# Residual adds shared out, Newton normalizers, a new meeting of two counting passes, and a causal mask added by VectorE behind the passes

## What is computed

```
h = relu(layernorm(x)); x = x + L0(h)   # two graph convolutions, then LSTMs over windows of 1, 2, 3, 4 nodes
h = relu(layernorm(x)); x = x + L1(h)   # graph attention: leaky scores, masked where adj == 0, softmax
h = relu(layernorm(x)); x = x + L2(h)   # attention: scores = q k^T * scale + adj, causal mask -1e30, softmax
h = relu(layernorm(x)); x = x + L3(h)   # U = eigenvectors of the normalized Laplacian of adj
                                        # out = U (relu(U^T h W1 + b1) W2 + b2)
```

## Time and profile before

| | us |
|---|---|
| median of 3 runs (879.49 to 884.33) | 883.62 |
| the profiled execution | 882.39 |
| its span, first to last instruction | 880.4 |
| TensorE busy / VectorE busy | 772.6 (88%) / 709.2 (81%) |
| ScalarE busy / GpSimd busy | 503.6 (57%) / 173.2 (20%) |
| granted TensorE clock, mean | 0.963 of full |

### The profile page before, as it was taken

One profiled execution on the slowest core, in us unless ns is written; L12 is line 12 of the kernel. 1 busy time (PEld: TensorE's weight loads), 2 busy tenths in 40 slices (PEclk: granted clock), 3 DMA queues, 4 the chain that ended last, 5 costly groups with the idle time before them and its releaser, 6 DMA issues. The chain is left out here.

```text
span 880.4 us, 13711 instructions
## 1 busy us (share of the span) xinstructions
PE 772.6 (88%) x3730; PEld 512.6 (58%) x3738; DVE 709.2 (81%) x3425; ACT 503.6 (57%) x1115; POOL 173.2 (20%) x398
## 2 busy tenths in 40 slices
PE   4699989999999999999999996688866887788998
PEld 3578854445445666665545545466645565566665
DVE  6888779999877889888888879778879899869433
ACT  0288956654443444444334331388755786698775
POOL 3111112222121221122122100012122322270000
PEclk9999999999999999999999999699997999899999
DMA  9100000000000000000000000000000000000122
GB/s 272 51 3 1 1 1 2 0 1 1 1 1 1 1 1 1 0 1 1 1 0 1 0 1 1 0 1 1 1 1 1 1 1 1 0 1 1 48 73 72
DMA packets 13970, 12.16 MB, mean 14 GB/s; under 512 B 1091, under 2 KB 10822, under 8 KB 13894
## 3 DMA queue, kind: packets, MB, share of 16 engines
q1 hardware_dynamic: 10992, 8.47, 3.3%
q10 hardware_dynamic: 2902, 2.82, 1.1%
HBM read 7.10 MB, written 4.19 MB: 13 GB/s over the span
## 5 line engine op out<-in xcount | busy, mean ns | idle before, releaser
L592 ACT ACTIVATE G<-bank,bias 128x512 f32<-128x512 f32 (+1 forms) x252 | 158.5, 633 | 181.5 <-PE bank L689 161.9
L689 PE MATMUL bank<-HT,wih 128*128 128x512 f32 (+1 forms) x504 | 246.0, 575 | 0.4 <-ACT HT L578 0.4
L441 POOL TENSOR_TENSOR col_root<-sa,neg_half 128x1 f32<-128x1 f32 x126 | 69.0, 548 | 409.6 <-DVE sa L936 409.6
L689 PE MATMUL bank<-H,whh 128*128 128x512 f32 (+1 forms) x288 | 137.6, 560 | 1.3 <-DVE H L934 0.8
L532 ACT COPY T<-bank 128x512 f32<-128x512 f32 x128 | 75.0, 586 | 55.2 <-PE bank L689 38.6
L528 ACT ACTIVATE T<-X,nbias,rstd 128x128 f32<-128x128 f32 x256 | 104.5, 484 | 3.0 <-DVE nbias L935 3.0
L689 PEld LDWEIGHTS bank<-HT,wih 128*128 128x128 f32 x504 | 81.0, 193 | 16.8 <-issue 10.2
L689 PEld LDWEIGHTS bank<-VI 128*128 128x128 f32 x254 | 45.0, 196 | 76.6 <-DVE VI L934 57.0
L689 PEld LDWEIGHTS bank<-XI,A 128*128 128x128 f32 x252 | 44.6, 197 | 57.4 <-DVE A L935 48.7
L699 PE MATMUL bank<-ident,T 128*128 128x128 f32 x256 | 40.9, 291 | 38.8 <-ACT T L635 32.6
L935 DVE SCALAR_TENSOR_TENSOR XI<-xy,bank 128x2 f32<-128x2 f32 x125 | 28.2, 225 | 43.3 <-PE bank L689 35.2
(11 more groups left out here) (350 smaller groups left out, 1664.9 us busy)
## 6 DMA issues: line engine op xcount, KB each, us to landing
out_x<-T SPq DMA_DIRECT2D x16, 256.0 KB, 2.3
wih<-in_WihT ACTq DMA_DIRECT2D x1, 1024.0 KB, 12.6
whh<-in_WhhT ACTq DMA_DIRECT2D x1, 1024.0 KB, 18.3
qkvT<-in_WqkvT ACTq DMA_DIRECT2D x1, 192.0 KB
wg<-in_Wg ACTq DMA_DIRECT2D x2, 64.0 KB
l3w<-in_L3W ACTq DMA_DIRECT2D x2, 64.0 KB
adj<-in_adj SPq DMA_DIRECT2D x1, 64.0 KB, 1.9
adjT<-in_adjT ACTq DMA_DIRECT2D x1, 64.0 KB
```

Source lines behind the costliest of these rows:

```text
L441: e.tensor_tensor(out=col["root"][:, :], in0=sa[:, 0:1], in1=neg_half[:, :], op=ALU.pow).then_inc(root_ready, 1)
L592: e.activation(G[x.h][:, gate, 0:n], gate_bank(k)[:, 0:n], ACT.Tanh if gate == 2 else ACT.Sigmoid, bias=bias[:, 4 * (x.p - 1) + gate:4 * ( ...
L689: mm = lambda out, l, r, start=True, stop=True: e.matmul(out, l, r, start=start, stop=stop)
```

## The change

- `half_list` has seven empty halves ahead in place of three, and no statistics in it. 45 attention halves are done by the end of the second pass, before and after.
- The residual adds: VectorE keeps groups 0, 3, 6, 9, 12 and 15. For the ten others ScalarE copies the bank to a tile of `T` and GpSimd adds that to `X`. VectorE takes `bn_stats` of all 16, in the order `RESIDUALS`. TensorE may turn the first groups before the last LSTM result stands. GpSimd's first tables now stand behind its ten adds.
- `normalizers` makes `rstd` on VectorE: an integer seed from the bits of the variance and three Newton steps. Statistics 3 to 7 use it; their square roots on ScalarE are gone. An exponential of one column in the residual stage (`warm`) loads ScalarE's table early.
- At the meeting of the passes one half is done ahead of the counts, one while TensorE forms the histogram, then statistics 4 and two halves ahead of step 0 of the second pass; the second pass has no place at step 2. The signs and sums of the first three blocks of each pass are put one slot later than `slot_of_block` gives, and within the slot ahead of the norm of a later group.
- For the nine groups whose scores come behind the passes (23 to 31) TensorE leaves out the mask product. VectorE makes, graph by graph, the negated sum of scores and `cmask` into `T`, with its minimum over the row as the bias; ScalarE's exponential reads `T` with scale -1.
- The parts of `tridiagonal` stand at other places among the last LSTM pieces.

The diff, cut to its core; its pieces are, in order, the lists, GpSimd's adds, ScalarE's copies and dropped roots, TensorE's mask product, and VectorE's functions.

```diff
-    halves = [("none", 0)] * 3
+    halves = [("none", 0)] * 7
...
+STATISTICS = {HALF.index(("scores", NG // 2 * m + 1)): m + 3 for m in range(1, 4)}
...
-    return 2 if step % n in places else 0
+    return 2 if step % n in places and (ps == 0 or step > n) else 0
...
+def on_vector(g):
+    return g % 3 == 0
+RESIDUALS = (0, 3, 1, 6, 2, 4, 9, 5, 7, 12, 8, 10, 15, 11, 13, 14)
+MASKED_BY_VECTOR = min(k for k in range(NG, GROUPS) if HALF.index(("scores", k)) >= block_ends()[-1] + 2)
-    BLOCKS_AFTER.setdefault(slot_of_block(_n), []).append(_n)
+    BLOCKS_AFTER.setdefault(slot_of_block(_n) + (_n % NB < NB - 1), []).append(_n)
...
+            for g in range(NG):
+                if not on_vector(g):
+                    xg = X[:, ds(g * GB, GB), :]
+                    e.wait_ge(st_c, copied_on_scalar(g))
+                    e.tensor_tensor(out=xg, in0=half4(turned_residual(g)), in1=xg, op=ALU.add).then_inc(st_g, 1)
...
+            def residual_copies(groups):
+                for g in groups:
+                    if not on_vector(g):
+                        e.wait_ge(st_T, g + 1)
+                        copy(turned_residual(g), bank[4 + g % 4], st_c)
+                if k == 1:
+                    e.activation(warm[:, :], half[:, :], ACT.Exp)
-            root(3)
-                if S in ROOTS_AFTER:
-                    root(ROOTS_AFTER[S])
-                if not it:
-                    root(7)
...
-                if nx:
+                if nx and nx.k < MASKED_BY_VECTOR:
                     mask = gmask if nx.gat else cmask
                     mm(half4(bk[2]), ident[:, :], mask[:, :].unsqueeze(1).to_broadcast([P, GB, P]), stop=False)
...
+            def normalizers(n):
+                o = COLUMNS[n]
+                variances(n)
+                net(e.tensor_scalar(rstd[:, o].bitcast(U32), var[:, o].bitcast(U32), -0.5, 1597463007.0, ALU.mult, ALU.add))
+                for _i in range(3):
+                    net(STT(dm[:, o], var[:, o], -0.5, rstd[:, o], ALU.mult, ALU.mult))
+                    net(TT(dm[:, o], dm[:, o], rstd[:, o], ALU.mult))
+                    net(STT(rstd[:, o], dm[:, o], 1.5, rstd[:, o], ALU.add, ALU.mult))
+                STT(nbias[:, o], mean[:, o], -0.5, rstd[:, o], ALU.mult, ALU.mult).then_inc(ln_rdy, 1)
...
+            def masked_scores(g):
+                e.wait_ge(q_s, g + 1)
+                for b in range(GB):
+                    i = e.tensor_tensor_reduce(out=T[g % 2][3][:, ds(b * P, P)], in0=bank[3 * (g % 2) + 2][:, ds(b * P, P)], in1=cmask[:, :], scale=-1.0, scalar=3e38,
+                                               op0=ALU.add, op1=ALU.min, accum_out=sm[g % 2][:, 4 + b:5 + b])
+                i.then_inc(q_m, 1)
...
+                    statistics(halves)
+                    for _i in range(2):
+                        attentions(halves)
+                        halves += 1
```

More of the change, by code:

```diff
@@ L268, in products @@
 def products(n):
-    return sum(2 if i % NB == NB - 1 else len(CUTS[i // NB]) - 1 for i in range(n + 1))
+    return sum(len(CUTS[i // NB]) - 1 for i in range(n + 1) if i % NB < NB - 1)
 def slot_of_block(n):
@@ L279, in slot_of_block, with added_on_vector, copied_on_scalar, turned @@
     return max(S for S in SLOTS if needs(S) <= reach)
+def on_vector(g):
+    return g % 3 == 0
+def added_on_vector(g):
+    return sum(on_vector(h) for h in range(g + 1))
+def copied_on_scalar(g):
+    return sum(not on_vector(h) for h in range(g + 1))
+def turned(k):
+    return range(3 * k, min(3 * k + 3, NG))
+RESIDUALS = (0, 3, 1, 6, 2, 4, 9, 5, 7, 12, 8, 10, 15, 11, 13, 14)
 HIST_IN = slot_of_block(NB - 1)
+MASKED_BY_VECTOR = min(k for k in range(NG, GROUPS) if HALF.index(("scores", k)) >= block_ends()[-1] + 2)
 LAMBDA_AFTER = slot_of_block(len(POINTS) * NB - 1) + 1
@@ L801, in residual_turns @@
             def residual_turns(k):
-                for g in range(3 * k, min(3 * k + 3, NG)):
-                    if g >= 4:
-                        e.wait_ge(st_x, g - 3)
+                for g in turned(k):
+                    if g == 0:
+                        e.wait_ge(l_h, HALF_OF_UNITS)
+                    if g == NG // 2:
+                        e.wait_ge(l_h, len(UNITS))
+                    if g < 3:
+                        e.wait_ge(l_act, gates_through(4 + g))
+                    if g == 3:
+                        e.wait_ge(wy_ac, 1)
+                    if g >= 4 and on_vector(g - 4):
+                        e.wait_ge(st_x, added_on_vector(g - 4))
+                    if g >= 4 and not on_vector(g - 4):
+                        e.wait_ge(st_c, copied_on_scalar(g - 4))
                     for b in range(GB):
@@ L1066, in _, with statistics @@
             inverted = {}
+            def statistics(h):
+                if h in STATISTICS:
+                    normalizers(STATISTICS[h])
             def attentions(h):
@@ L1077, in attentions @@
                     gat_scores(x.g)
-                if kind == "scores" and not x.gat:
+                if kind == "scores" and not x.gat and k < MASKED_BY_VECTOR:
                     att_scores(x.g)
+                if kind == "scores" and k >= MASKED_BY_VECTOR:
+                    masked_scores(x.g)
                 if kind == "output" and x.gat:
@@ new lines, in _ @@
+                made_y = link.note(TS(y, bank[1][:, 0:1], c("root"), c("signed"), ALU.mult, ALU.mult))
+                made_a1 = link.note(TS(c("a1"), c("size"), c("root"), 1.0, ALU.mult, ALU.add))
+                e.wait_ge(ch_e, made_u)
+                TT(v, u, xi[:, 2:3], ALU.add).then_inc(p_ready, 1)
+                e.wait_ge(ch_e, made_y)
+                TT(p, y, bank[1][:, 1:2], ALU.add).then_inc(p_ready, 1)
+                e.wait_ge(ch_e, made_a1)
+                made_gam = link.note(e.reciprocal(out=gam, in_=c("a1")))
@@ L1259, in _ @@
                         half_next = half_behind(ps, b * KB + s)
+                        if half_next:
+                            statistics(halves)
                         if s == KB - 1:
@@ L1298, in _ @@
                         rec(STT(uu[0][:, 0:f], uu[0][:, 0:f], ne2p[:, P // 2:P // 2 + 1], uu[1][:, 0:f], ALU.mult, ALU.add))
-                        TT(v4(prodL, KB, f)[:, KB - 1, 1], uu[0][:, 0:f], tt[:, 0:f], ALU.mult).then_inc(pr_ready, 1)
-                for _i in range(2):
-                    attentions(halves)
-                    halves += 1
+                        TT(v4(prodL, KB, f)[:, KB - 1, 1], uu[0][:, 0:f], tt[:, 0:f], ALU.mult).then_inc(pl_ready, 1)
+                statistics(halves)
+                attentions(halves)
+                if ps:
+                    attentions(halves + 1)
                 e.wait_ge(sum_ps, NB * (ps + 1))
@@ L1316, in _ @@
                 link(TS(c("cnt1"), c("cnt1"), 1.0, 1.0, ALU.max, ALU.subtract))
+                halves += 2
                 if ps < len(POINTS) - 1:
@@ L1456, in _ @@
                 halves += 1
-            stats_2(7)
+            normalizers(7)
             for it in range(NG // 2):
```

189 lines of the change are left out of this document (90 added, 99 removed).

## The result

The changed kernel takes **854.68 us** (median of four runs, 853.95 to 857.29) where the kernel before takes 882.32 (four runs, 879.49 to 884.33): a ratio of 0.969 with an interval of 0.966 to 0.973. A repeat with other runs of both gave 857.0 against 882.3, 0.971 (0.969 to 0.974). Three executions of the study, two of r6 and the profiled one of r9, took 902 to 2546 us in a slow state and are left out of every median here.

What follows compares the result with a forecast made beforehand. VectorE was taken to bound the residual stage and second pass, chains through the engines part of the rest; -6.5 - 14 - 3.5 + 4 + 1 = -19 gave 863.4 by the profile, 864.6 us against the median, range 856 to 873.

Steps and rivals of the forecast that it cites:

- Residual stage, -6.5: Residual stage: VectorE sets the end and has ten adds fewer, 6.5 us less (bounds -7.5 and -3).
- the fourth rival: Residual stage: each of GpSimd's ten adds holds VectorE 1.27 us, +12.7, so 876 us; chance 0.04.
- First pass, -14: First pass: less attention work and fewer waits for VectorE, 14 us less (bounds -18 and -8).
- I leave 5 of the 14.8 us, because ScalarE was as full as VectorE: First pass: 5 of VectorE's 14.8 us of waits were expected to stay, a gain of 9.8 us.
- The meeting, -3.5: Meeting of the passes: earlier signs and an output moved behind the counts, 3.5 us less (bounds -4.5 and 0).
- The output behind the counts: Meeting: the moved output, 1.8 us, was to fit the 2.03 us wait for the histogram.
- Second pass, +4: Second pass: more halves and Newton steps, less hold-ups that go, 4 us more (bounds 0 and +9).
- One place less, so waits +0.8: Second pass: with one place less, the waits were to grow by 0.8 us.
- Behind the passes, +1: Stretch behind the passes: mask work on VectorE, a root gone, Newton steps added; 1 us more (bounds -7 and +9).
- The pair: Behind the passes: VectorE's masked minimum from a bank with its accumulator read, taken at 0.33 us a graph.
- TensorE paces: Behind the passes: nine mask products saved, 7.7 us, come out in full, so 856 us; chance 0.08.
- The level: Whole kernel: 1.2 us added to the profile's 863.4 to reach the median's level, 864.6 us.

Runs made afterwards that it cites:

- r6: Changed kernel with the output of the meeting ahead of the counts again instead of behind them: 857.2 us, ratio 0.971.
- r9: Changed kernel with GpSimd waiting for `M` before its first residual add: 853.3 us, ratio 0.967; it left no usable trace.
- r3: Changed kernel with all sixteen residual adds on VectorE in order 0 to 15, no ScalarE copies or GpSimd adds: 859.24 us, ratio 0.974.
- r14: The kernel of r9 (changed kernel, GpSimd's residual adds behind `M`) run once more for its trace: 855.18 us, ratio 0.968.
- r5: Changed kernel with three empty halves ahead of the attention instead of seven: 863.92 us, ratio 0.979.
- r11: Changed kernel with nine empty halves ahead of the attention instead of seven: 858.86 us, ratio 0.973.
- r13: Changed kernel with the signs and their sums back at their old place, except at the end of a pass: 870.7 us, ratio 0.985.
- r4: Changed kernel with unused one-column square roots on ScalarE at the three places behind which the half statistics stand: 864.26 us, ratio 0.978.
- r16: Kernel before with only the signs and their sums moved one group later, and the separate semaphore for the last products: 876.53 us, ratio 0.994.
- r2: Changed kernel with the nine causal mask products back on TensorE and plain maxima on VectorE: 854.21 us, ratio 0.967.

## Why the prediction was wrong, by its own steps

*Residual stage, -6.5: right in size.* From `M` on it measured -6.2 to -6.9, and the adds alone 6.5 (r3). VectorE's bank adds and statistics did not stretch beside GpSimd, as the earlier trace rows said; here are twelve statistics and a bank add of the changed kernel, while GpSimd adds two groups from 540.74 to 543.26:

```profile
539.95 2.42 DVE L976 BATCH_NORM_STATS2 stat<-X 128x6 f32<-128x128 f32 x12
542.29 0.68 DVE L968 TENSOR_TENSOR X<-bank,X 128x512 f32<-128x512 f32 x1
```

What had no term is `M` itself, 2.0 us late behind two held-up copies. With all adds on VectorE it stands 1.0 us earlier than before (r3), with the split 1.1 later, so the stage as a whole gives 5.1 to 5.8. That GpSimd's adds stop VectorE's adds (the fourth rival) fell; they stop its copies. The prediction took from the Trainium skill (SBUF — State Buffer, Who interferes with whom) only what it says of instructions with two inputs in SBUF. The page also says that copies can enter a mode that takes the ports shared with GpSimd, and that the later of the two then blocks for the whole instruction. The rows 1.26 and 1.19 agree with it: these copies, 0.20 us each alone, cost 2 us, and r14 gives them back. In which mode they ran no run shows.

*First pass, -14: measured -15.6, with two errors that part cancelled.* "I leave 5 of the 14.8 us, because ScalarE was as full as VectorE": 0.6 were left. Against it, VectorE's hold-ups beside GpSimd's tables rose from 1.0 to 4.1 us, for which the sum had no term. They come with the late start, in which VectorE runs recurrence steps while the tables are written: with three empty halves they are 1.0 us (r5), with nine 5.6 (r11). Here are two of them:

```profile
571.32 0.76 DVE L968 TENSOR_TENSOR tt<-HT,G 128x64 f32<-128x64 f32 x1
572.00 1.30 DVE L968 TENSOR_TENSOR uu<-HT,n 128x64 f32<-128x64 f32 x1
```

Waits -14.2, halves -4.3 (the prediction's figure), hold-ups +3.2 make -15.3. ScalarE's busy share said nothing of whether it paced: besides, it stood in line for GpSimd for 3.8 us.

*The meeting, -3.5: measured -4.0, by another way.* The output behind the counts gives nothing (r6), where 1.8 us were expected, so the size is right by chance. The signs now start 0.3 us behind the last write of products, not 3.6, and the counts stand 2.0 us behind it, not 5.8. That the root that went made this room is argued; no run puts it back here.

```profile
619.27 0.19 DVE L968 TENSOR_TENSOR prodL<-uu,tt 128x32 f32<-128x32 f32 x1
```

```profile
619.55 1.06 ACT L654 ACTIVATE sg<-prodL 128x1024 bf16<-128x1024 f32 x1 [0.22 <-DVE prodL L968]
```

*Second pass, +4: measured +0.9.* The step that failed here is "One place less, so waits +0.8": they fell by 3.2. The hold-ups fell by 2.1 (9.5 to 7.4) where -3.7 stood, and by the rest of the balance the halves and Newton steps cost some 6.2 where 6.9 stood. Two things bring the waits back: the signs' old place, with 6.2 us of waits and a pass 5.7 longer (r13), and the roots, with 2.8 us of waits and 1.8 longer (r4). The sum had neither in this pass.

*So the step that failed is one that the sum did not have:* the signs and their sums one group later. The diff showed it, and the prediction costed the root that went from beside it, but not the place. It is worth 5.3 us on the kernel before (r16) and 9 to 14 where the rest of the change is made (r13). The roots, costed at 2.8 us for one, are worth 6.1 in the traces for three (r4), and the late start 6.8 (r5).

*Behind the passes, +1: measured -0.9.* The pair costs 0.21 us, the low end, not 0.33: 2.3 us less for groups 27 to 31. The root behind the passes is worth 4.2 (r4), not 2.8. With these two the sum would be at -2.7; why 1.8 of it did not come is not shown. The floor of 26.2 us at the twist, which the sum did not have, can only have capped what is won ahead of it. The rival "TensorE paces", which gave 856 and so the nearest number, is wrong in its mechanism: with the products back the kernel is not slower (r2). On the table load the rows of r4 repeat: 1.28 us each, exponentials 2.8 us behind the first load, no drain. So a drain is not what makes the root dearer; the waits for outputs in the loop that it hits are (9.0 us for 3.6), though the 5.3 us that follow from the Trainium skill (ScalarE: Activation LUTs, What ACT_TABLE_LOAD costs) would have come nearer to the 4.2.

*The level.* 1.2 us were added because the profiled execution of before lay below its median then; with a fourth run it lies on it. Of the 9.9 us between forecast and result, 5.8 to 6.7 are terms and 1.2 is this step; the scatter of the loop is large enough for the rest.

## What to carry to other kernels

When an edit moves an instruction that waits for a third engine within an in-order queue, give the place its own term: list what it waits for, when that is made, and who is queued behind it; here a cheap move was worth 5.3 us alone, more than the mask or the meeting. Before taking work off an engine in a stretch, look for the chain that nothing in the stretch can shorten (the 26.2 us of the twist), for it caps every gain that lies ahead of its end. And cut the trace at landmarks behind the part that scatters: most stretches of the changed kernel repeat within 0.1 us where medians of this kernel differ by 2.3.

## What the runs showed of the hardware that was not expected

- A VectorE copy of 128x64 from SBUF to SBUF took 1.26 and 1.19 us beside GpSimd's adds and 0.20 without them (r3, r14), while bank adds (0.68) and statistics (0.87 for four) ran undisturbed beside them.
- A masked maximum over a bank with its accumulator read costs 0.21 us of VectorE by spacing, no more than a sum of squares in SBUF.
- A root of one column on ScalarE that nobody waits for cost 4.2 us in a stretch where load, root and load last 2.8.
